# Gather passes of a graph network: ScalarE's exponent or absolute value ahead of its item work

## What is computed

```python
# layer 0
h_src = h[src]
edge_feats = jnp.abs(h[dst] - h_src)
new_h = jnp.concatenate([h_src, edge_feats], axis=-1) @ W_edge.T + b_edge
seg_sum = jax.ops.segment_sum(new_h, dst, num_segments=n)
# layer 1, twice
att = jnp.einsum('ehd,ehd->eh', q[dst], k[src]) / scale
ex = jnp.exp(att - m[dst])
s = jax.ops.segment_sum(ex, dst, num_segments=n)
msg = (v[src] * alpha[:, :, None]).reshape(-1, D)
aggr = jax.ops.segment_sum(msg, dst, num_segments=n)
```

## Time and profile before

| | us |
|---|---|
| median of 3 runs | 7105.87 |
| lowest, highest | 7094.47, 7110.97 |
| the profiled execution | 7118.68 |
| its span (first to last instruction) | 7116.9 |
| VectorE busy in the span | 4436.3 |
| GpSimd busy in the span | 3117.5 |
| ScalarE busy in the span | 2920.9 |

### The profile page before, as it was taken

One profiled execution on the slowest core, in us unless ns is written; L12 is line 12 of the kernel. 1 busy time (PEld: TensorE's weight loads), 2 busy tenths in 40 slices (PEclk: granted clock), 3 DMA queues, 4 the chain that ended last, 5 costly groups with the idle time before them and its releaser, 6 DMA issues. The chain is left out here.

```text
span 7116.9 us, 123314 instructions
## 1 busy us (share of the span) xinstructions
PE 5456.4 (77%) x28313; PEld 3639.5 (51%) x28314; DVE 4436.3 (62%) x13076; ACT 2920.9 (41%) x5625; POOL 3117.5 (44%) x3096
## 2 busy tenths in 40 slices
PE   7987986777777556666666756666666899999998
PEld 3443444666665544554554545555554444444433
DVE  9999987777776567877777478888885311100000
ACT  2543543777776225555555425555553200000000
POOL 3754753777775016666665017777771000000000
PEclk9999997999999779889887878888887899999999
DMA  1000002555556116666667016666663477777799
GB/s 23 0 3 1 0 21 86 174 171 172 172 172 149 37 64 200 199 199 197 199 196 169 4 56 199 193 192 195 193 193 63 154 288 288 271 288 289 290 423 385
DMA packets 464533, 1168.30 MB, mean 164 GB/s; under 512 B 112062, under 2 KB 175102, under 8 KB 432156
## 3 DMA queue, kind: packets, MB, share of 16 engines
q1 hardware_dynamic: 337228, 892.75, 33.8%
q0 software_dynamic: 124928, 273.12, 16.1%
q10 hardware_dynamic: 2256, 0.89, 0.1%
HBM read 759.86 MB, written 405.30 MB: 164 GB/s over the span
## 5 line engine op out<-in xcount | busy, mean ns | idle before, releaser
L720 POOL DMA_INDIRECT ACC<-tab_kv,STAGE x1664 | 1661.5, 999 | 1430.3 <-DMA STAGE<-IDX 730.6
L1242 ACT ACTIVATE PS<-PS,X 128x512 f32<-128x512 f32 x1456 | 968.5, 665 | 525.2 <-PE PS L926 503.9
L914 PE MATMUL PS<-SCR 128*128 128x137 f32 x3328 | 596.7, 330 | 707.5 <-DVE ACC L1742 691.2
L720 POOL DMA_INDIRECT SCR<-tab_h,STAGE x832 | 827.6, 995 | 346.5 <-issue 274.4
L914 PEld LDWEIGHTS PS<-SCR 128*128 128x128 f32 x3328 | 496.3, 220 | 852.6 <-DVE ACC L1742 798.7
L1742 DVE TENSOR_TENSOR ACC<-ACC,PS 128x137 f32 (+1 forms) x2288 | 747.8, 327 | 247.7 <-PE PS L918 131.6
L1083 PE MATMUL PS<-ACC,Q 128*128 128x512 f32 (+3 forms) x2548 | 844.3, 577 | 49.5 <-DMA ACC<-adj 40.0
L787 PE MATMUL PS<-Q 128*128 128x416 f16 x4160 | 756.8, 340 | 60.9 <-DVE Q L1536 60.9
L896 PEld LDWEIGHTS PS<-Q,SCR 128*128 128x128 f32 x4992 | 712.5, 212 | 171.8 <-issue 146.8
L896 PE MATMUL PS<-Q,SCR 128*128 x4992 | 752.9, 299 | 59.2 <-issue 51.6
L681 POOL DMA_INDIRECT placed<-ACC,X x576 | 606.4, 1053 | 408.2 <-DVE X L1513 219.6
(11 more groups left out here) (297 smaller groups left out, 7481.6 us busy)
## 6 DMA issues: line engine op xcount, KB each, us to landing
ACC<-adj SPq DMA_DIRECT2D x252, 1792.0 KB, 6.8
adj<-X SPq DMA_DIRECT2D x936, 256.0 KB
adj<-ITEM SPq DMA_DIRECT2D x520, 256.0 KB
ACC<-tab_kv,STAGE POOLq DMA_INDIRECT x1664
SCR<-tab_h,STAGE POOLq DMA_INDIRECT x832
tab_kv<-SCR SPq DMA_DIRECT2D x14, 896.0 KB, 4.1
ACC<-adj SPq DMA_DIRECT2D x21, 448.0 KB, 4.1
placed<-ACC,X POOLq DMA_INDIRECT x576, 2.2
```

The costliest lines, as they stand in the source:

```text
L720: nc.gpsimd.indirect_dma_start(G[:, q, j, 0:w], None, table, bass.IndirectOffsetOnAxis(STAGE[:, u, q * S4 + j:q * S4 + j + 1], 0))\
L914: ins = nc.tensor.matmul(dst, oh, M[:, u % 2, j, :], start=True, stop=True)
L1242: nc.scalar.activation(CLASS_SUM[(k + 1) % 2], CLASS_SUM[k % 2], ACT.Copy, scale=KEEP[:, bass.ds(i, 1)])\
```

## The change

ScalarE's body for a group becomes: exponent or absolute value first; then the third item of the group before, if it has one; then the copy for the group two ahead; then the group's first two items. In "att1", where no group has a third item, only the order of exponent, copy and items is other. A third item that the last group of a pass might have would follow the loop. The other engines' instructions stay in their order. A variable is renamed from `before` to `passes`.

```diff
@@ body(it, u) of ScalarE's edge_pass @@
                 def body(it, u):
                     gi = it * 4 + u
-                    own = items_of(name, it, u)
-                    if exists(gi + 2):
-                        copy(it if u < 2 else it + 1, (u + 2) % 4)
-                    item(it, *own[0])
+                    before = (it, u - 1) if u else (it - 1, 3)
                     wait(act, s, "att", gi + 1)
                     if kind == "att":
                         wait(act, s, "agg", gi - 1)
...
                     else:
                         nc.scalar.activation(M[:, u % 2, :, 0:D], PROD[:, :, :], ACT.Abs).then_inc(s["msg"], 1)
-                    for each in own[1:]:
+                    if not (isinstance(gi, int) and gi == 0):
+                        for each in items_of(name, *before)[2:]:
+                            item(before[0], *each)
+                    if exists(gi + 2):
+                        copy(it if u < 2 else it + 1, (u + 2) % 4)
+                    for each in items_of(name, it, u)[0:2]:
                         item(it, *each)
...
                 per_group(act, body)
+                for each in items_of(name, GROUPS // 4 - 1, 3)[2:]:
+                    item(GROUPS // 4 - 1, *each)
```

More of the change, by code:

```diff
@@ L1232, in edge_pass @@
                 base, per, ring = PLAN[name]
-                before = PASSES.index(name)
-                used = sum(sum(p) // r for _, p, r in [PLAN[k] for k in PASSES[:before]]) * (STEPS // PB)
+                passes = PASSES.index(name)
+                used = sum(sum(p) // r for _, p, r in [PLAN[k] for k in PASSES[:passes]]) * (STEPS // PB)
                 turn = sum(per) // ring
@@ L1261, in body @@
                         nc.scalar.activation(M[:, u % 2, :, 0:D], PROD[:, :, :], ACT.Abs).then_inc(s["msg"], 1)
-                    for each in own[1:]:
+                    if not (isinstance(gi, int) and gi == 0):
[4 more added lines that the diff above has]
+                    for each in items_of(name, it, u)[0:2]:
                         item(it, *each)
-                act.wait_ge(ad["opened"], before + 1)
-                if before:
+                act.wait_ge(ad["opened"], passes + 1)
+                if passes:
                     ins = nc.scalar.activation(CLASS_SUM[0], KEPT, ACT.Copy)
@@ L1274, in edge_pass @@
                 per_group(act, body)
-                if before < 2:
+                for each in items_of(name, GROUPS // 4 - 1, 3)[2:]:
+                    item(GROUPS // 4 - 1, *each)
+                if passes < 2:
                     last = base + sum(per) * STEPS // PB
-                    act.wait_ge(ad["kept"], last + before + 1)
+                    act.wait_ge(ad["kept"], last + passes + 1)
                     act.wait_ge(stored[2], 16 * (used + turn * (STEPS // PB)))
```

## The result

| | before | after |
|---|---|---|
| median of 4 runs, us | 7107.14 | 6859.33 |
| lowest, highest | 7094.47, 7110.97 | 6853.69, 6862.35 |
| span of the profiled execution | 7116.9 | 6851.9 |
| TensorE's mean granted clock | 0.911 | 0.922 |

The ratio is 0.9653, with a 95% interval of 0.9637 to 0.967: 248 us or 3.5% faster. The direction was right and the size was not.

What follows compares the result with a forecast made beforehand. Gathers were taken to nearly bound "diff" and "att1", and the other engines' loop, VectorE busiest, to pace "att0". Gains of 22, 12 and 100 us summed to 134 us, giving 6972 us, range 6915 to 7045.

Steps and rivals of the forecast that it cites:

- floor: In the gather passes, four gathers at 0.995 + 0.30 us each were claimed to need 5.18 us per group.

## What to carry to other kernels

When two engines run at nearly the same pace, being close to one's floor does not show that it is the limit: look at who waits for whom, and price the edit by the wait that it removes on the busiest engine, not by the wait of the engine behind it. That gave 126 and 53 us here for gains of 137 and 61; in "diff", where the wait was TensorE's and gathers came next, 77 us of wait gave 50. Divide a wait by the stretch that it was read over. A duration that contains collisions with another engine is not a floor, since the edit changes the collisions (the mean gather of "diff", 0.995 us, came to 0.967). Put an operation that other engines' critical work waits for ahead of bulk copies in its queue, but keep it from standing behind something that waits for a third engine: with half the gathers, the copy ahead of the absolute value made "diff" 1255.4 us long instead of 1041.2.

## What the hardware showed unexpectedly

**A gather's length depends on when it starts.** Timeline of "diff", the kernel before and then the kernel after; in each the one-hot and the gather that starts while it runs, and in the second also a gather that had started ahead of a one-hot:

```profile
1702.12 0.68 DVE L1724 TENSOR_TENSOR SCR<-IOTA,LO 128x512 f32<-128x512 f32 x1
1702.44 1.18 POOL L720 DMA_INDIRECT SCR<-tab_h,STAGE  x1 [0.75 <-PE PS L918]
```

```profile
1700.88 0.94 POOL L720 DMA_INDIRECT SCR<-tab_h,STAGE  x1 [0.30 <-PE PS L918]
...
1701.13 0.68 DVE L1728 TENSOR_TENSOR SCR<-IOTA,LO 128x512 f32<-128x512 f32 x1
...
1717.38 0.68 DVE L1728 TENSOR_TENSOR SCR<-IOTA,LO 128x512 f32<-128x512 f32 x1
1717.49 1.39 POOL L720 DMA_INDIRECT SCR<-tab_h,STAGE  x1 [0.30 <-issue]
```

Counted over all gathers of the three passes of both kernels: one that was already running when a one-hot began lasts 0.944 to 0.946 us on average and never over 0.97. One that starts while a one-hot runs lasts 1.05 to 1.23 us on average in the six passes. The earlier it starts in the one-hot, the longer it lasts (kernel before): 1.42 us in the first tenth of a microsecond, 1.16 in the fourth, 0.95 once 0.6 us have gone. In "diff" 132 gathers started so before, with a mean of 1.135 us, and 57 after, with 1.047. That makes up 19 of the 22 us by which the gathers of this pass became shorter, with a change that touches neither them nor VectorE.

It depends on the operation. The message product, with two inputs in SBUF like the one-hot, does the same (1.36 us for 11 gathers in its second tenth, before). A gather that starts while VectorE's subtraction L1771 runs (one input in PSUM, 42 gathers) or its reduction L1783 (one input, 227 gathers) lasts 0.942 to 0.947 us. The items' fp16 one-hots L1750 lengthen it a little, to 1.04 us in their second tenth.

So for these one-hots the order of starting decides: a gather that is ahead of the one-hot keeps its 0.944 to 0.946 us, and one that starts in the first tenth of a microsecond of the one-hot takes 1.42. The one-hots are not longer for a gather: the 393 that began while a gather ran lasted 0.684 us on average before the change, as did the 14 with no gather near. What makes it so the counts do not show.

**Two chips of the same kind differed by 23% on the same kernel**, 7107 and 8712 us or more. The traces on the slower ones have stops of VectorE and ScalarE that are booked under no engine; whether the chip or something beside it makes them is not known. The change was worth 3.5% on one and cost 0.6% on the other. How the kernel before stands on the same chip has to be looked at ahead of any ratio.
